# A two-layer transformer kernel: the prelude's order, the layer-0 quantisation moved into the second run

## What is computed

```python
def _L0_ffn_ref(x, weight, ln_gamma, ln_beta):
    ...
    mu = jnp.mean(x, axis=-1, keepdims=True)
    var = jnp.var(x, axis=-1, keepdims=True)
    xn = (x - mu) * jax.lax.rsqrt(var + LN_EPS) * ln_gamma + ln_beta
    beta = jnp.mean(jnp.abs(weight))
    w_q = jnp.clip(ste_round(weight / (beta + EPS)), -1.0, 1.0)
    gamma = jnp.max(jnp.abs(xn))
    xq = jnp.clip(xn * QB / gamma, -QB + EPS, QB - EPS)
    y = jnp.einsum('bsd,du->bsu', xq, w_q)
    return y * (gamma * beta / QB)
...
xn = _layernorm(x, axis=-1)
x = x + _L0_attn_ref(xn, ...) + _L0_ffn_ref(xn, ...)
xn = _layernorm(x, axis=-1)
x = x + _L1_attn_ref(xn, ...) + _L1_ffn_ref(xn, ...)
```

## Time and profile before

| what | value |
|---|---|
| median of 3 runs | 2063.88 us |
| the profiled execution | 2064.26 us |
| its span | 2062.5 us |
| TensorE busy (PE) | 1859.0 us, 90% |
| VectorE (DVE) | 1689.8 us, 82% |
| ScalarE (ACT) | 1711.0 us, 83% |
| GpSimd (POOL) | 1106.7 us, 54% |
| mean granted TensorE clock | 0.977 |

### The profile page before, as it was taken

One profiled execution on the slowest core, in us unless ns is written; L12 is line 12 of the kernel. 1 busy time (PEld: TensorE's weight loads), 2 busy tenths in 40 slices (PEclk: granted clock), 3 DMA queues, 4 the chain that ended last, 5 costly groups with the idle time before them and its releaser, 6 DMA issues.

```text
span 2062.5 us, 48350 instructions
## 1 busy us (share of the span) xinstructions
PE 1859.0 (90%) x16166; PEld 1503.4 (73%) x16288; DVE 1689.8 (82%) x3449; ACT 1711.0 (83%) x2256; POOL 1106.7 (54%) x1212
## 2 busy tenths in 40 slices
PE   1266999999999999999999999999999999999986
PEld 1144777777777777777777777777777777778765
DVE  5558888888898888888988888889888888888851
ACT  5414889888888898888888888988888889888887
POOL 5524556665555566655555666555566655554432
PEclk9678999999999999999999999999999999999999
DMA  6333233223332232233323322332233223322110
GB/s 158 99 85 77 63 78 89 65 67 87 85 87 61 72 87 64 67 86 86 81 60 79 87 64 67 85 87 76 58 87 85 62 71 85 87 68 64 44 45 6
DMA packets 302343, 155.16 MB, mean 75 GB/s; under 512 B 14389, under 2 KB 298325, under 8 KB 302293
## 3 DMA queue, kind: packets, MB, share of 16 engines
q1 hardware_dynamic: 302292, 154.52, 29.7%
HBM read 82.64 MB, written 71.30 MB: 75 GB/s over the span
## 4 chain that ended last, share of the span: by engine, by line
PE 58%; DVE 23%; issue 11%; ACT 5%; SPq 1%; POOL 1%; DVEq 1%; DMA 0%; ACTq 0%; POOLq 0%
PE pu L1748 8%; DVE zc L888 5%; PE pu L1566 4%; PE pav L1566 4%; PE pu L1600 4%; PE pav L1623 3%; PE pav L1600 3%; PE pu L1623 3%; PE pav L1574 2%; PE pm L1730 2%; PE pm L1643 2%; PE pu L1586 2%; PE pav L1626 1%; PE pav L1738 1%; PE pav L1739 1%
## 5 line engine op out<-in xcount | busy, mean ns | idle before, releaser
L1183 POOL TENSOR_TENSOR zs<-zc,zs 128x1024 f32<-128x1024 f32 x192 | 450.7, 2361 | 134.2 <-ACT zc L1408 134.2
L1096 POOL TENSOR_TENSOR rs<-ve,mhalf 128x2 f32<-128x2 f32 x64 | 45.3, 708 | 407.1 <-DVE ve L673 404.3
L1748 PE MATMUL pu<-hid,h1t 128*128 128x256 f32 x1024 | 243.5, 381 | 0.0
L1748 PE MATMUL pu<-hid,h2t 128*128 128x256 f32 x1024 | 237.7, 380 | 0.0
L1407 ACT ACTIVATE zs<-zc,mhalf 128x1024 f32<-128x1024 f32 x192 | 218.4, 1138 | 0.4
L1408 ACT ACTIVATE zc<-zc,phalf 128x1024 f32<-128x1024 f32 x192 | 217.9, 1135 | 0.0
L1566 PE MATMUL pu<-k_st,q_st 128*128 128x256 bf16 (+1 forms) x1152 | 170.9, 253 | 42.5 <-DVE zc L888 16.4
L1748 PEld LDWEIGHTS pu<-hid,h2t 128*128 128x128 f32 x1024 | 187.1, 190 | 23.3 <-DVE zc L888 0.3
L1432 ACT ACTIVATE zs<-zs 128x1024 f32<-128x1024 f32 x192 | 201.4, 1049 | 2.0
L1748 PEld LDWEIGHTS pu<-hid,h1t 128*128 128x128 f32 x1024 | 186.1, 192 | 21.2
L1426 ACT ACTIVATE zs<-zs 128x1024 f32<-128x1024 f32 x192 | 197.4, 1044 | 0.0
(11 more groups left out here) (277 smaller groups left out, 5257.4 us busy)
## 6 DMA issues: line engine op xcount, KB each, us to landing
scr<-parts SPq DMA_DIRECT2D x256, 192.0 KB, 2.4
q_st<-scr SPq DMA_DIRECT2D x128, 256.0 KB, 3.9
scr<-parts SPq DMA_DIRECT2D x128, 128.0 KB, 2.4
k_st<-scr SPq DMA_DIRECT2D x64, 256.0 KB
k_st<-scr SPq DMA_DIRECT2D x32, 512.0 KB, 5.1
x<-in_L_attn_x SPq DMA_DIRECT2D x32, 128.0 KB, 3.3
out<-xold SPq DMA_DIRECT2D x32, 128.0 KB, 1.8
q_st<-m_t SPq DMA_DIRECT2D x128, 4.0 KB
```

What stands on the lines that cost most here:

```text
L1183: G.tensor_tensor(zs[:, c], zc[:, c], zs[:, c], ALU.add).then_inc(sum_done.sem, 1)
L1748: last = PE.matmul(u.ap[:, c * T:(c + 1) * T], w[:, k, c * P:(c + 1) * P], src[:, k, :], start=(k == 0), stop=(k == HC - 1))
```

## The change

It does the following.

- **SP.** The `first` list is issued in three batches: 8 loads ahead of chunk 2, 8 ahead of chunk 3, 6 behind it. It now also holds `lat_least` and `w_out0`, which were in `rest`. `stack_maxima` comes before the `rest` loads.
- **GpSimd.** `split0` comes first after the norms of sequence 0, then all four chunks' powers, then the wait for the `first` loads and the residual. The reductions over the partitions, `scaled_weights` and the clip leave the opening. The clip of sequence 0 (`clip_first`) stands in the second run behind the last window, ahead of `split0`.
- **ScalarE.** Sequence 0's plain input goes to `xa_first`, which is the memory of `x1res`, and the second run's `xa_t` waits for no clip. `clear(1)` comes ahead of the chunks, and chunk 3 is normalised behind `shift_part`.
- **VectorE.** `chunk_extremes(0)` stands ahead of `latent_gates`, `chunk_extremes(1)` behind the maxima. `wcol` and `gcol` are also spread over 128 columns (in `wn` and `wr`). In the second run stand `ternary_weights` (behind `latent_norm`), `layer1_weights` (behind `mix`) and `deep_weights` (h1, h2, w3, behind `values0`).
- **TensorE.** `extremes_t` in the second run, between the last scores and attend, transposes the two spread columns into a bank it shares with the projections of q and k, so that VectorE can reduce along rows.

```diff
@@ sync, opening
-                for c in range(PRE_CHUNKS):
+                batches = [], first[:8], first[8:16], first[16:]
+                for c in (0, 1, 2, 3):
+                    if c > 1:
+                        for dst, src in batches[c - 1]:
+                            sp.dma_start(dst, src).then_inc(first_in, 16)
                     sp.dma_start(px[c].rearrange("p (n d) -> p n d", d=D), x_chunk[c]).then_inc(pre_in[c], 16)
-                for dst, src in first:
+                for dst, src in batches[-1]:
                     sp.dma_start(dst, src).then_inc(first_in, 16)
...
                 load_x(run.norm.index())
+                stack_maxima(run, run.first)
                 for dst, src in rest:
                     sp.dma_start(dst, src).then_inc(rest_in, 16)
-                stack_maxima(run, run.first)
@@ vector
-                V.tensor_reduce(out=wcol[:], in_=w_tern, axis=AX_X, op=ALU.add, apply_absolute_value=True).then_inc(cols_ready, 1)
+                pre(V.tensor_reduce(out=wcol[:], in_=w_tern, axis=AX_X, op=ALU.add, apply_absolute_value=True))
+                V.tensor_copy(wn, bc(wcol[:], [P, P])).then_inc(cols_ready, 1)
...
+                pre(V.tensor_reduce(out=gcol[:], in_=pall.rearrange("p e d -> p (e d)"), axis=AX_X, op=ALU.max, apply_absolute_value=True))
+                V.tensor_copy(wr, bc(gcol[:], [P, P])).then_inc(cols_ready, 1)
+
+            def deep_weights():
+
+                for w, scale in ((h1t, r3), (h2t, r4)):
+                    V.tensor_tensor(w[:], w[:], bc(scale.unsqueeze(1), [P, HC, HID]), ALU.mult)
+                V.tensor_tensor(w3t[:], w3t[:], bc(s3.unsqueeze(1), [P, HC, D]), ALU.mult)
...
-            def ternary_weights():
-
-                dve.wait_ge(all_ready, 2)
+            def ternary_weights(run):
+
+                u = misc(run, "extremes")
+                u.wait_full(dve)
+                V.tensor_reduce(out=wall[:], in_=u.ap[:, 0:P], axis=AX_X, op=ALU.add)
+                pre(V.tensor_reduce(out=gall[:], in_=u.ap[:, P:2 * P], axis=AX_X, op=ALU.max))
+                dve.sem_inc(u.free, 1)
@@ vector, iteration
                     latent_norm(run, link[M])
+                if run.quantise:
+                    ternary_weights(run)
...
                     mix(m, link[M])
+                if run.quantise:
+                    layer1_weights()
...
                     values0(run, f)
+                if run.quantise:
+                    deep_weights()
@@ gpsimd
-            def scaled_weights():
-
-                pool.wait_ge(rest_in, 16 * len(rest))
-                for w, scale in ((h1t, r3), (h2t, r4)):
-                    G.tensor_tensor(w[:], w[:], bc(scale.unsqueeze(1), [P, HC, HID]), ALU.mult)
+            def clip_first(m):
+
+                pool.wait_ge(weights_ready, 1)
+                G.tensor_scalar(xq_t[:], xa_first, thr[:], nthr[:], ALU.min, ALU.max).then_inc(xq_ready.sem, 1)
...
-                chunk_scales(0)
+                split0(f, Links(pool, pool_link[F], f))
+                for c in range(PRE_CHUNKS):
+                    chunk_scales(c)
                 pool.wait_ge(first_in, 16 * len(first))
                 residual0(run, f)
-                split0(f, Links(pool, pool_link[F], f))
-                chunk_scales(1)
-                chunk_scales(2)
-                chunk_scales(3)
@@ scalar
-                act.wait_ge(xq_ready.sem, xq_ready.at(f, 0))
-                S.activation(xa_t[:], u.ap[:, T:2 * T], ACT.Identity, bias=bet_col[:], scale=gam_col[:]).then_inc(u.free, 1)
+                if not run.quantise:
+                    act.wait_ge(xq_ready.sem, xq_ready.at(f, 0))
+                S.activation(plain, u.ap[:, T:2 * T], ACT.Identity, bias=bet_col[:], scale=gam_col[:]).then_inc(u.free, 1)
@@ tensor
+            def extremes_t(run):
+
+                u = misc(run, "extremes")
+                u.wait_free(pe)
+                pe.wait_ge(cols_ready, 2)
+                PE.transpose(u.ap[:, 0:P], wn, ident[:])
+                PE.transpose(u.ap[:, P:2 * P], wr, ident[:]).then_inc(u.full, 1)
```

More of the change, by code:

```diff
@@ L122, in __init__ @@
         self.t0, self.trips, self.stages = t0, trips, stages
+QUANTISE = 1
 LAG = {"norm": -1, "first": 0, "middle": 1, "last": 2, "end": 3, "out": 4}
@@ L132, in pipeline_phases @@
     at_work = lambda t: tuple(n for n, lag in LAG.items() if 0 <= t - lag < NB)
-    single = lambda t: Phase(t, 1, at_work(t))
+    single = lambda t: Phase(t, 1, at_work(t) + (("weights",) if t == QUANTISE else ()))
     head, tail = range(min(LAG.values()), deepest + 1), range(NB - 1, NB + deepest)
@@ L145, in __init__ @@
         self.phase, self.t = phase, t
+        self.quantise = "weights" in phase.stages
         self.norm, self.first, self.middle, self.last, self.end, self.out = (Sequence(t, LAG[n]) if n in phase.stages else None for n in LAG)
@@ L326, in build @@
         AV_USES = uses(M, ["exp1", "exp5"]) + uses(L, ["min1"]) + uses(M, ["exp3", "av0"]) + uses(E, ["sub0", "sub2", "sub4"]) + uses(F, ["max1"]) + uses(L, ["min5"]) + uses(F, ["max3", "max5"]) + uses(M, ["f1_0"])
-        MISC_USES = [uses(O, ["yffn"]) + uses(F, ["qk"]) + uses(E, ["mT1"]) + uses(F, ["v"]) + uses(M, ["qkv1a"]) + uses(F, ["rqkv"]) + uses(E, ["yT"]),
+        MISC_USES = [uses(O, ["yffn"]) + uses(F, ["qk"]) + uses("weights", ["extremes"]) + uses(E, ["mT1"]) + uses(F, ["v"]) + uses(M, ["qkv1a"]) + uses(F, ["rqkv"]) + uses(E, ["yT"]),
                      uses(F, ["xT"]) + uses(M, ["lexp", "lo", "rem", "mixT", "y0", "x1T", "qkv1b", "embT"]) + uses(F, ["lmax", "mT"]) + uses(E, ["y1"])]
@@ L346, in build @@
         pool_pre = sem("pool_pre")
-        cols_ready, all_ready = sem("cols_ready"), sem("all_ready")
+        cols_ready = sem("cols_ready")
         weights_ready = sem("weights_ready")
@@ L441, in build @@
         first = [
-            (b_out0[:], row(A["L0_attn_out_b"])),
             (w_rq[:], A["L0_attn_rq_w"]), (b_rq[:], col(A["L0_attn_rq_b"])), (w_rkv[:], A["L0_attn_rkv_w"]),
@@ L445, in build @@
         ] + given("lat_rows", "lat_cols", "lat_ones", "ident_bf", "win0", "win1", "winl") + [
+            (b_out0[:], row(A["L0_attn_out_b"])), (lat_least[:], A["lat_least"]), (w_out0[:], A["L0_attn_out_w"]),
             (w_rout[0:LD, 0:D], A["L0_attn_rout_w"]), (w_rout[LD:2 * LD, 0:D], A["L0_attn_rout_w"]), (b_rout[:, 0:D], row(A["L0_attn_rout_b"])),
@@ L452, in build @@
             (w_qkv1[:], A["L1_attn_W_qkv"]), (b_qk1[:], row(A["L1_attn_b_qkv"][0:2 * D])), (b_v1[:], row(A["L1_attn_b_qkv"][2 * D:3 * D])),
-            (w3t[:], A["w3t"].rearrange("(c p) n -> p c n", p=P)), (s3, row(A["L1_ffn_w3_s"])), (w_out0[:], A["L0_attn_out_w"]),
+            (w3t[:], A["w3t"].rearrange("(c p) n -> p c n", p=P)), (s3, row(A["L1_ffn_w3_s"])),
             (r3, row(A["L1_ffn_h1_s"])), (r4, row(A["L1_ffn_h2_s"])),
             (h1t[:], A["h1t"].rearrange("(c p) n -> p c n", p=P)), (h2t[:], A["h2t"].rearrange("(c p) n -> p c n", p=P)),
-        ] + given("lat_least", "cau0", "sel") + [
+        ] + given("cau0", "sel") + [
             (w_out1[:], A["L1_attn_W_out"]), (b_out1[:], row(A["L1_attn_b_out"])), (w_sur[:], row(A["L1_attn_w_sur"])),
@@ L1051, in opening @@
                 shift_lo(run, "mT", 0, f)
+                chunk_extremes(1)
                 chunk_extremes(2)
@@ L1227, in iteration @@
                     window(run, 3)
+                if run.quantise:
+                    clip_first(m)
                 if l:
@@ L1276, in opening @@
                 normed_again(a)
-                pool.wait_ge(cols_ready, 1)
-                G.partition_all_reduce(wall[:], wcol[:], P, RADD).then_inc(all_ready, 1)
-                pool.wait_ge(cols_ready, 2)
-                G.partition_all_reduce(gall[:], gcol[:], P, RMAX).then_inc(all_ready, 1)
-                scaled_weights()
-                pool.wait_ge(weights_ready, 1)
-                clip_input(run, f)
             opening(*opening_runs)
@@ L1314, in _, with transposes0 @@
             LOG_EXP, SQRT, GELU = "natural_log_exp_and_others", "sqrt_and_others", "gelu_and_others"
-            def transposes0(run, f):
+            def transposes0(run, f, plain):
                 u = misc(run, "xT")
@@ L1461, in iteration @@
                 if f:
-                    transposes0(run, f)
+                    transposes0(run, f, xa_t[:])
                 if m:
@@ L1539, in opening @@
                 act.wait_ge(early_in, 16 * len(early))
-                transposes0(run, f)
+                transposes0(run, f, xa_first)
                 operands0(run, f)
-                for c in range(PRE_CHUNKS):
-                    chunk_normed(c)
+                clear(1)
+                chunk_normed(0)
+                chunk_normed(1)
+                chunk_normed(2)
                 shift_part(run, "mT", 0)
-                clear(1)
+                chunk_normed(3)
             opening(*opening_runs)
@@ L1808, in iteration @@
                     scores_by_key(unit(run, "exp3"), 3)
```

(2 more changed lines are left out.)

10 lines of the change are left out of this document (2 added, 8 removed).

## The result

The changed kernel takes **2042.28 us** (median of 4 runs, 2040.78 to 2045.01) against 2064.26 for the kernel before beside it: ratio 0.9895, 95% interval 0.9878 to 0.9912. A second set of four runs gave 2040.00 (2039.14 to 2041.40), ratio 0.9881 (0.9865 to 0.9898). Faster, as forecast, but 4.4 to 6.7 us less so than the 2035.6 predicted; the first median lies 0.28 us outside the range, the second inside.

What follows compares the result with a forecast made beforehand. TensorE bounds the steady part; the prelude stalls on late stacking and the clip holding xa_t's buffer. -31.2+1.7+1.7 = -27.8, -0.5 for the clock: 2064.26-28.3 = 2036.0, 0.38 less for the median: 2035.6; range 2030.0 to 2042.0.

Steps and rivals of the forecast that it cites:

- The stall goes whole: Second run: xa_t no longer waits for the clip, prob_l starts at 69.8 instead of 101.05: -31.2, all except 0.7.
- Stacking at 26.5: Opening, SP's queue: with an early split and small loads between chunks, stacking starts at 26.5, 12.1 us earlier.
- rival 1: SP's queue or chunks later: stacking and chunk 3 slip 3 to 6 us, total 2038.5 to 2041.5; chance 0.17.
- one of the signs of being wrong: SP's queue: the forecast is wrong if stalls above 1 us show at more than two small loads.
- Reductions at 49.5: Opening: VectorE's reductions of the first maxima end at 49.5, between 48.7 and 49.8: -12.9.
- `xf` stays beside VectorE's extremes, 12.7 us from the first power as before: Opening, GpSimd: the next sequence's xf takes as long as before and is ready at 63.2.
- +1.7 and +1.7: Second run: column maxima by TensorE cost 1.7 before the gate logits; scalings on VectorE cost 1.7 before v_new.
- The weights' chain: Second run, VectorE from thr to w_qs, done at 79.65; o_t copies queue behind it, so gate logits lose 1.7.
- Queue order: Opening, SP: small loads issued between chunks help start the stacking at 26.5, while chunk 3 lands near 26.5, not 22.
- split ahead of powers: Opening, GpSimd: the split takes 3.2 us and is done near 19.6, after which SP is late next.
- Later runs only shift: Runs after the prelude: they keep the gain, since each stage hangs on another and no absolute date is left.
- -0.5 for TensorE's clock: Second run: less idle before TensorE's products keeps it more at its fast rate, worth 0 to 1 us.

Runs made afterwards that it cites:

- the buffer alone: Kernel before, with only sequence 0's plain input moved to x1res, so the second run's xa_t waits for no clip: 2065.96 us (1.0010).
- the early extremes: Changed kernel with VectorE doing chunk 1's extremes ahead of latent_maxima, not behind the maxima: 2039.30 us (0.9871).
- run 3: Not an experiment: a pipeline run inside the kernel, numbered by its prob_l, which starts at 219.02 before; the changed kernel leads by 23.3 and 26.3 us.
- run 8: Not an experiment: a later pipeline run, numbered by its prob_l, which starts at 511.90 before; the changed kernel leads by 21.8 and 24.5 us.
- run 1: Not an experiment: the prediction's second run, numbered by its prob_l, which starts at 101.05 before; the changed kernel leads by 26.6 and 27.5 us.
- one swapped line: power(rs1) ahead of residual0 in GpSimd's iteration: 2027.29 us on the changed kernel (0.9818), 2049.81 on the kernel before (0.9919).

## Why the prediction came out as it did

- *The stall goes whole* was right: `xa_t` without a wait; the reductions, their idle time and the scalings left the path. The experiment with the buffer alone shows that the wait for the buffer is not enough, the one with the reductions back on GpSimd that they are 3 to 5 us of it. The clip's new place and the scalings weren't taken apart.
- *Stacking at 26.5* failed by 1.4 to 1.9: the sum had one stalled small load and a stalled last chunk, which together brought it to 22 where the last chunk was through at 22.14 to 22.51. The queue stalls at three small loads instead (3.74, 2.09, 1.48 in the first execution), and the third of them was in no term. That is rival 1 in mechanism, 2 to 3 us with what follows, and it is one of the signs of being wrong that I had named.
- *Reductions at 49.5*: 51.4 to 52.2. The lateness of the stacking, and 0.5 because TensorE's products stayed slow (0.63 for what later took 0.38) through three units and a part of the fourth. The granted clock of that stretch is 1.00, so what makes them slow isn't shown.
- *`xf` stays beside VectorE's extremes, 12.7 us from the first power as before* is the step that failed most by itself: 15.2. Two chunks lay beside it before, three now; I had moved chunk 1's extremes behind the maxima in the same paragraph and not priced what they do to GpSimd. Shown by the early extremes (12.5). It took VectorE's place as what is late: `prob_l` waited 1.93 for TensorE. Of the 3.7 to 4.6 us that `prob_l` came late, this is 1.9; the other 1.8 to 2.7 are VectorE's lateness, that of the stacking and the maxima.
- *+1.7 and +1.7*: from `prob_l` to `v_new` the lead shrank by 3.3 in both executions, against 3.4. That the sum came out is in part luck. The weights' chain was put at 1.7 and had cost 0.8 at `rsum`. At `x` 1.9 was gone, since in between `gr` took 1.10 us beside the next split, in place of 0.43, which was in no term. From there to `v_new` it was another 1.4, with `deep_weights` at 1.1 by the experiments and not 1.7, though its products took 2.28, against 2.26. (In three of the experiments, in which `gr` isn't held up, `rsum` comes 11.5 us behind `prob_l`, just as forecast, and not 10.6; why that stretch has two lengths isn't shown.)
- *Queue order* and *split ahead of powers*: worth about 2 and 0. That the first buys time was right, of the second I had said only that SP is late next, which holds.
- *Later runs only shift* failed: 1.5 to 1.8 us went between run 3 and run 8, nearly all of it because the long periods, in which GpSimd's `xres` holds up VectorE's `ve`, begin three runs sooner. No absolute date was needed for that; a near tie of two engines is enough.
- *-0.5 for TensorE's clock* did not come: the granted clock was 0.83 and 0.70 in the halves of run 1 before, 0.76 and 0.77 after.
- The whole, in the profiled executions. Forecast: 31.2 at `prob_l`, 27.8 behind the second run, 28.3 with the clock. First execution: 26.6, then 3.3 less by run 3, 1.5 less by run 8, 2.5 less in the tail: 19.3 (2045.01). Second: 27.5, 1.2 less, 1.8 less, 0.6 more from there to the end: 25.1 (2039.14). So 3.7 to 4.6 us are the head's, 1.5 to 1.8 the hold's, and the rest is what differs between executions, with either sign, which my range left out: it held bounds for costs, none for the clock.

## What to carry over

When work is taken off one engine's path and another's is moved, price the pairs that will then run side by side, not only each engine's sum: here the slow `xf` and the longer periods, and with them 3.4 to 3.7 us at `prob_l` and in the later runs, were VectorE and GpSimd side by side; the other misses were SP's queue (1.4 to 1.9) and the clock. Where a pipelined loop's period changes and its work doesn't, look for a near tie of two engines: comparing a short and a long period instruction by instruction found this one, and one swapped line was worth 13 to 16 us, over half of what the whole prelude change gave.
